# Mixture of experts on one core: leftover single tiles get units of their own at four fixed places

## The reference, cut to what matters

```
logits = flat @ gate_w.T                       # (4096, 8)
top_vals, top_idx = jax.lax.top_k(logits, 2)
top_w = jax.nn.softmax(top_vals, axis=-1)
for e in range(8):
    hdn = gelu(flat @ w1[e] + b1[e])           # 256 -> 1024
    out = out + combine[:, e:e+1] * (hdn @ w2[e] + b2[e])   # 1024 -> 256
```

## Time and profile before

| | us |
|---|---|
| median of 3 runs (lowest to highest) | 782.21 (781.34 to 785.01) |
| the profiled execution | 781.53 |
| its span, first to last instruction | 779.7 |
| stage A, about | 0 to 216 |
| stage B, about | 222 to 328.5 |
| stage C, about | 329.5 to 779.7 |
| PE busy over the span | 713.2 (91%) |

### The profile page before, as it was taken

How to read it: one execution, slowest core, us unless ns; L and a number is a source line. 1 busy time by engine, 2 the same in 40 slices (tenths; PEclk the granted TensorE clock), 3 DMA queues, 4 the chain that set the end, 5 groups by cost and what they waited for, 6 DMA issues and landing times.

```text
span 779.7 us, 18458 instructions
## 1 busy us (share of the span) xinstructions
PE 713.2 (91%) x5438; PEld 676.9 (87%) x5439; DVE 440.9 (57%) x1047; ACT 331.9 (43%) x640; POOL 407.9 (52%) x480
## 2 busy tenths in 40 slices
PE   5899999999948888489999999999999999999993
PEld 4899898998926666389999999999999999999993
DVE  3675756756636999735445455455454454454551
ACT  2673755747515677332323323323323223233230
POOL 1474565787662443273555546546555555555233
PEclk9999999999969999599999999999999999999997
DMA  7759568497460333224557536665576276273122
GB/s 243 247 174 398 208 264 359 163 333 252 171 271 28 111 110 109 84 75 120 170 156 229 178 55 206 186 176 148 155 246 166 41 237 175 48 229 77 19 29 30
DMA packets 45873, 130.14 MB, mean 167 GB/s; under 512 B 5185, under 2 KB 35521, under 8 KB 41217
## 3 DMA queue, kind: packets, MB, share of 16 engines
q1 hardware_dynamic: 30560, 104.86, 36.3%
q0 software_dynamic: 13904, 19.45, 14.6%
q10 hardware_dynamic: 1360, 5.24, 1.7%
HBM read 186.80 MB, written 47.59 MB: 301 GB/s over the span
## 4 chain that ended last, share of the span: by engine, by line
PE 55%; issue 1%; DMA 0%; POOL 0%; DVE 0%; ACT 0%; POOLq 0%; DVEq 0%
PE ps_h L73 9%; PE ps_h L74 9%; PE ps_h L75 9%; PE ps_y L73 8%; PE ps_y L75 8%; PE ps_y L74 8%; PE ps_x L1596 2%; PE ps_y L1589 1%; DMA out_tok<-y,to_row 0%; POOL out_tok L1471 0%; DVE xtl L1531 0%; DVE yb L1551 0%; DVE y L1558 0%; ACT xth L1496 0%; POOL to_row L1467 0%
## 5 line engine op out<-in xcount | busy, mean ns | idle before, releaser
L1505 ACT ACTIVATE g<-ps_h,bias 128x256 f32<-128x256 f32 x288 | 120.8, 471 | 277.7 <-PE ps_h L75 277.7
L1471 POOL DMA_INDIRECT out_tok<-y,to_row x72 | 126.9, 1763 | 137.7 <-DVE y L1558 117.2
L73 PE MATMUL ps_h<-xth,wbuf 128*128 128x256 f32 x576 | 163.2, 283 | 3.3 <-issue 1.8
L73 PE MATMUL ps_y<-wbuf,gl 128*128 x576 | 164.6, 286 | 0.0
L74 PE MATMUL ps_h<-xtl,wbuf 128*128 128x256 f32 x576 | 163.1, 283 | 0.0
L75 PE MATMUL ps_h<-xth,wbuf 128*128 128x256 f32 x576 | 161.8, 281 | 0.0
L75 PE MATMUL ps_y<-wbuf,gh 128*128 x576 | 161.7, 281 | 0.0
L74 PE MATMUL ps_y<-wbuf,gh 128*128 x576 | 161.7, 281 | 0.0
L73 PEld LDWEIGHTS ps_h<-xth,wbuf 128*128 128x128 f32 x576 | 108.0, 188 | 3.7 <-issue 2.1
L75 PEld LDWEIGHTS ps_h<-xth,wbuf 128*128 128x128 f32 x576 | 109.6, 190 | 0.0
L74 PEld LDWEIGHTS ps_y<-wbuf,gh 128*128 128x128 f32 x576 | 108.8, 189 | 0.0
(11 more groups left out here) (239 smaller groups left out, 1284.9 us busy)
## 6 DMA issues: line engine op xcount, KB each, us to landing
wbuf<-wsplit SPq DMA_DIRECT2D x71, 2048.0 KB, 8.1
wsplit<-wbuf SPq DMA_DIRECT2D x14, 2048.0 KB, 11.9
wraw<-in_w SPq DMA_DIRECT2D x16, 1024.0 KB, 7.9
raw<-in_x_ch ACTq DMA_DIRECT2D x5, 1024.0 KB, 8.8
normed<-x SPq DMA_DIRECT2D x8, 528.0 KB, 3.0
tok<-in_x_tok SPq DMA_DIRECT2D x1, 4096.0 KB, 16.7
out_tok<-tok SPq DMA_DIRECT2D x8, 512.0 KB, 3.7
x_rows<-normed,from_row POOLq DMA_INDIRECT x72, 3.4
```

The lines of the kernel that those rows point to most:

```text
L73: eng.matmul(out, ll, rh, start=first, stop=False)
L1471: pool.indirect_dma_start(out=out, out_offset=bass.IndirectOffsetOnAxis(ap=to_row[:, par, s:s + 1], axis=0), in_=y[:, par, s, :], in_offse ...
L1505: last = act.activation(g[:, f, :], ps_h[:, q, f % 2, :], ACT.Gelu_apprx_tanh, bias=bias1[:, bass.ds(e, 1), f:f + 1].rearrange("p a f -> p ...
```

## The change

Each expert's number of pairs becomes its count divided by 256 and rounded (count + 127, shifted by 8, at least 1), and where 1 to 128 tokens are left over, they are one **lone** tile. For the counts above: 3, 4, 4, 3, 4, 5, 5, 4 pairs = 32 and 1, 0, 1, 1, 0, 0, 0, 1 lone tiles = 4. The usual run still has 36 units, but every eighth (units 7, 15, 23 and 31) is a lone unit of one tile, whatever expert it belongs to, with both layers' weights in a buffer of its own, `lone_w` (128 x 8192 float32). It is filled in four transfers of a quarter during the first four units of each period of eight. What does not fit 32 pairs and 4 lone tiles runs in ten more units behind the branch. To make room, `x`, `g`, `y` and `yb` of stage C lie in the token buffer of the stages before. The loop body has eight units and runs three times.

```diff
+PERIOD = 8
+LONE = PERIOD - 1
+LONES = E // 2
+FULL = 2 * TOK // PAIR
+USUAL = FULL + LONES
...
 # stage B, SyncE: the second layers of experts 0 and 1 go to wsplit too
             sp.dma_start(bias1[:, :, :], b1_t).then_inc(biases_in, 16)
+            for e in range(2):
+                sp.dma_start(wsplit[e, :, W2AT:WROW], wbuf[:, e, W2AT:WROW].bitcast(F32)).then_inc(second_out, 16)
...
 # stage B, GpSimd: the pair number of each unit's place, three iotas for one
-                    (tile_id[:, :], [[1, PAIRS]], 0, 0),
+                    (by_period[:, :, 0:LONE], [[LONE, LONES], [1, LONE]], 0, 0),
+                    (by_period[:, :, LONE], [[LONE, LONES]], LONE - 1, 0),
+                    (tile_id[:, LONES * PERIOD:REST], [[1, REST - LONES * PERIOD]], LONES * LONE, 0),
...
 # stage C, SyncE
+            def lone_weights(u, at):
+                layer, n = at // 2, W2AT // 2
+                e = entry(sp, T_EXPERT, u + (LONE - at), E - 1)
+                cols = slice(at * n, (at + 1) * n)
+                sp.dma_start(lone_w[:, cols].bitcast(F32),
+                             wsplit[bass.ds(e, 1)].rearrange("a p w -> (a p) w")[:, cols]).then_inc(lone_in[layer], 16)
...
+                    if at < 4 and not (isinstance(u, int) and u + LONE - at >= USUAL):
+                        lone_weights(u, at)
...
+                    wait_apart(sp, lone_set, 1)
...
 # stage C, VectorE, ahead of the first x_low
+            def lone_table():
...
+                then(dve.tensor_scalar(lone_tiles_i[:, :], count_i[:, :], P.bit_length() - 1, None, ALU.arith_shift_right))
+                then(dve.tensor_copy(lone_tiles[:, :], lone_tiles_i[:, :]))
...
+                for i in range(1, PAIRS - USUAL + 1):
+                    then(dve.tensor_scalar(buffer_f[:, i:i + 1], buffer_f[:, i - 1:i], -1.0, 1.0, ALU.mult, ALU.add))
+                dve.tensor_copy(tabs[:, T_BUFFER, USUAL:PAIRS], buffer_f[:, 1:PAIRS - USUAL + 1]).then_inc(lone_set, 1)
...
+                if lo == 0:
+                    lone_table()
+                x_low(lo, lo % PERIOD)
...
 # stage C, TensorE
-                for s in range(2):
+                for s in range(rows_of(u, at) // P):
                     for k in range(KT):
                         last = pe.transpose(ps_x[:, k, s * P:(s + 1) * P], x[:, slot, s, k * P:(k + 1) * P], ident[:, :])
...
+                both = lone_w[:, 0:W2AT] if alone(u, at) else wbuf[:, par, 0:W2AT]
...
-                            last = mm3(pe, ps_h[:, q, f % 2, :], (wh[:, k, rows], wl[:, k, rows]),
-                                       (xth[:, par, k], xtl[:, par, k]), k == 0, k == KT - 1)
+                            last = mm3(pe, ps_h[:, q, f % 2, 0:n], (wh[:, k, rows], wl[:, k, rows]),
+                                       (xth[:, par, k, 0:n], xtl[:, par, k, 0:n]), k == 0, k == KT - 1)
...
-                for s in range(2):
+                for s in range(rows_of(u, at) // P):
                     rows = slice(s * P, (s + 1) * P)
```

More of the change, by code:

```diff
@@ L694, in _, with stage_b @@
             images(pe, image)
-def stage_b(nc, sem, tok, wbuf, wsplit, ident, fixed, xn, tabs, bias1, bias2, records, normed, b1_t, b2, out):
+def stage_b(nc, sem, tok, wbuf, wsplit, ident, fixed, xn, tabs, bias1, bias2, records, count_i, n_pairs, ends,
+            expert, expert_id, normed, b1_t, b2, out):
     with ExitStack() as ctx:
@@ L743, in stage_b @@
         empty = sb("empty", [P, CELLS])
[L745 to L749, removed]
+        pairs_i = sb("pairs_i", [P, E], I32)
+        past, picked = sb("past", [P, REST, E]), sb("picked", [P, REST, E])
+        passed, starts, first = sb("passed", [P, REST]), sb("starts", [P, REST]), sb("first", [P, REST])
+        expert_i = sb("expert_i", [P, REST], I32)
         ps_out = ps("ps_out", [P, B, HALF])
@@ L1190, in make_table @@
                 dve.memset(tabs[:, T_CHANGED, 0:1], 0)
                 dve.tensor_scalar(tabs[:, T_CHANGED, 1:2], expert[:, 1:2], 0.0, None, ALU.is_gt)
[L1192 to L1196, removed]
+                dve.tensor_tensor(tabs[:, T_CHANGED, 2:REST], expert[:, 2:REST], expert[:, 0:REST - 2], ALU.is_gt)
@@ L1198, in decode @@
+                then(dve.tensor_copy(expert_i[:, :], expert[:, 0:REST]))
+                dve.tensor_scalar(tabs[:, T_BUFFER, 0:REST], expert_i[:, :], 1, None, ALU.bitwise_and)
+                then(dve.scalar_tensor_tensor(out=tabs[:, T_FIRST, 1:REST], in0=expert[:, 1:REST], scalar=float(E - 1),
+                                              in1=first[:, 1:REST], op0=ALU.is_lt, op1=ALU.mult))
             def decode():
@@ L1322, with stage_c @@
 T_EXPERT, T_COLUMN, T_FIRST, T_NEXT, T_BUFFER, T_TOTAL, T_CHANGED = range(7)
-def stage_c(nc, sem, wbuf, ident, tabs, bias1, bias2, records, wsplit, normed, out):
+def stage_c(nc, sem, room, wbuf, ident, tabs, bias1, bias2, records, count_i, n_pairs, ends, pair_experts, expert_id,
+            wsplit, normed, out):
     with ExitStack() as ctx:
@@ L1351, in stage_c @@
         share_d = sem("c_share")
+        lone_w = sb("lone_w", [P, WROW], F32R)
+        lone_in = [sem(f"c_lone_w{i + 1}_in") for i in range(2)]
+        lone_set, lone_step = sem("c_lone_table"), sem("c_lone_steps")
+        lone_tiles_i, lone_tiles = sb("lone_tiles_i", [P, E], I32), sb("lone_tiles", [P, E])
+        lone_ends, lone_column = sb("lone_ends", [P, E]), sb("lone_column", [P, E])
+        lone_past, lone_hit = sb("lone_past", [P, E, E]), sb("lone_hit", [P, E, E])
+        lone_expert, lone_at = sb("lone_expert", [P, E]), sb("lone_at", [P, E])
+        lone_total, buffer_f = sb("lone_total", [P, 2]), sb("buffer_f", [P, PAIRS - USUAL + 1])
         xh_d, xl_d, g_d = sem("c_x_high"), sem("c_x_low"), sem("c_g")
@@ L1387, in all_pairs, with alone, rows_of, periods @@
                 run(USUAL, PAIRS)
+        def alone(u, at):
+            return at % PERIOD == LONE and not (isinstance(u, int) and u >= USUAL)
+        def rows_of(u, at):
+            return P if alone(u, at) else PAIR
+        def periods(u, at):
+            return u // PERIOD if isinstance(u, int) else (u - at % PERIOD) // PERIOD
         def later(u, step):
@@ L1394, in entry, with before, loads_of_first_layer @@
             return eng.value_load(tabs[0:1, row, bass.ds(u, 1)], min_val=0, max_val=top)
[L1396 to L1402, removed]
+        def before(u, at):
+            return u // SLOT if isinstance(u, int) else (u - at % SLOT) // SLOT
+        def loads_of_first_layer(u, at):
+            return before(u, at) * (SLOT // 2) + (at % SLOT + 1) // 2
         block = ctx.enter_context(nc.Block())
@@ L1447, in _, with gather @@
                 pool.sem_inc(s, CREDIT)
-            def gather(u, slot):
+            def gather(u, at):
+                slot = at % SLOT
+                if at == LONE and isinstance(u, int) and u == LONE:
+                    wait_apart(pool, lone_set, 1)
                 column = entry(pool, T_COLUMN, u, COLS - 2)
@@ L1556, in result @@
                 dve.wait_ge(share_d, done(u))
-                for s in range(2):
+                for s in range(m):
                     last = dve.tensor_scalar(y[:, par, s, :], yb[:, s, :], share[:, slot, s:s + 1], None, ALU.mult)
@@ L1597, in turn_x, with layer1 @@
                 last.then_inc(xt_mm, 1)
-            def layer1(u, slot):
-                par = slot % 2
-                wh, wl = [wbuf[:, par, i * W2AT // 2:(i + 1) * W2AT // 2].rearrange("p (k n) -> p k n", k=KT) for i in range(2)]
+            def layer1(u, at):
+                par, n = at % 2, rows_of(u, at)
+                both = lone_w[:, 0:W2AT] if alone(u, at) else wbuf[:, par, 0:W2AT]
+                wh, wl = [both[:, i * W2AT // 2:(i + 1) * W2AT // 2].rearrange("p (k n) -> p k n", k=KT) for i in range(2)]
                 if later(u, 1):
-                    pe.wait_ge(w1_in[par], loads_of_first_layer(u, slot) * 16)
+                    pe.wait_ge(w1_in[par], loads_of_first_layer(u, at) * 16)
+                if alone(u, at):
+                    pe.wait_ge(lone_in[0], periods(u, at) * 32 + 32)
                 pe.wait_ge(xl_d, done(u))
```

227 lines of the change are left out of this document (152 added, 75 removed).

## The result

The changed kernel takes 785.79 us in the median (784.25 to 787.46, 20 runs), the kernel before, in turn with it on the same chip, 783.15 us (780.52 to 785.2, 20 runs). The ratio is 1.0035, with a 95% interval of 1.0026 to 1.0043: slower by 2.6 us, where 768 us and a gain were forecast. The profiled execution of the changed kernel has a span of 783.5 us (before: 779.7).

A forecast was written before the change was run, and what follows sets the result against it. TensorE's queue was taken to bound stage C; 4 x (3.08 + 0.48) = 14.2 us saved, 0.3 + 0.2 + 0.1 = 0.6 added, turning 781.5 into 768 us, range 760 to 776.

The forecast's parts named there:

- the loop: Stage C's loop: eight units instead of four means fewer turns, TensorE has no idle time there, cost 0.
- its signs of being wrong: Narrow matmuls starting over 0.13 or under 0.09 us apart, or TensorE idling beside the lone units.
- Narrow matmuls: Layer 1 of a lone unit, 128 columns instead of 256: 0.109 us per matmul, 0.48 us saved per unit.
- columns count: Rival: lone-unit layer 1 time follows columns, 0.060 us per matmul, 758.5 us, half-way 763; chance 0.10.
- narrow is slow: Rival: lone-unit layer 1 matmuls take 0.215 us each, as two passes, ending at 788.2 us; chance 0.17.
- The transposes' pace: Unit 3's 128-column transposes, 0.109 us apart at full clock, taken as the pace of lone-unit layer 1 matmuls.
- The other row that was to carry this: L601's 24-column matmuls, 0.217 us apart, read as lower clock and halved to support a floor set by weights.
- A lone unit: TensorE in stage C: 3.08 us saved in layer 2 and transposes, plus 0.48 in layer 1, per unit.
- No wait beside the lone units: Stage C: GpSimd not late, 0.95 us to spare before unit 9, cost 0; rival of new waits 772 to 776, chance 0.07.
- Weights: Lone units' weight transfers, 4 MB per period: DMA share rises to about 0.7, nothing waits, cost 0.
- The table of lone tiles: 41 small VectorE instructions before the first x_low, 7.2 us mostly hidden: 0 to 0.5 us added, 0.3 taken.
- Stage B: Two more iotas and longer records 0.2 us, make_table's longer steps below 0.1 us; the two 2 MB stores 0.

The follow-up runs named there:

- the long loop alone: Kernel before, only its loop body changed to eight units run three times instead of four run seven times: 797.13 us, ratio 1.0176.
- its two runs with the hint: Changed kernel with TensorE told ahead that the loop's backward branch will be taken, measured twice: 771.78 us (0.9864) and 771.24 us (0.9857).
- With the two missed terms out of the way: Changed kernel with TensorE told ahead of the loop's backward branch, and without the ten spare units and their branch: 768.72 us, ratio 0.9830.

## Why the prediction was wrong

**The step that failed** is the loop: it "has fewer turns; in the stretch of seven turns PE has no idle time, so 0". The rows were read rightly, but they belong to a body of four units. That a body twice as long goes back as cheaply was taken over from them without a bound. It costs 13.7 us by medians in the long loop alone, and about 14 as the difference between the changed kernel and its two runs with the hint. No rival named it, and the range had no room for it. Nor did any of its signs of being wrong come up: they watched the lone units' matmuls and waits, and not the loop. The short taken branch (0.25 us at most) shows what a branch costs when the code is at hand, and nothing of the case when it isn't. But a branch of microseconds stood in the trace before all the same, on the engine that sets the time: TensorE's own jump over the three spare units, at the end of its program, where nothing waits for it.

```profile
L1386 PEldq COMPARE_BRANCH  x1: 4076/4076/4076, 765.0 to 765.0; - x1
```

It took 4.1 us (after, over ten units, 4.2), where the same engine's taken branches in the loop of four took at most 0.25. No run here takes this jump apart, but as a bound for two ways back it gives an estimate of up to 8 us, before any loss by the clock, and not 0.

**A term was left out**: the jump over ten spare units instead of three at the end of GpSimd's program, 2.3 us in the trace. Taking all spare units out gives 2.5 back by medians and 2.9 in the trace, of which 0.6 is in the kernel before as well (7.7 against 7.1 us from the last scatter to the end).

**The rest of the sum held.** Saved between units 3 and 35, once the way back is hinted: 379.62 - 365.39 = 14.23 us, against 14.2 forecast. Its parts:
- Narrow matmuls: 0.111 us against 0.109, with nothing of "columns count" or "narrow is slow" in them, and 0.44 us saved per lone unit against 0.48. The transposes' pace was the right row to take. The other row that was to carry this does not: L601 was read as running at the lower clock, and half its 0.217 us was taken. But the trace before has the granted clock at 1.00 there (start and end of the stretch, then as in the rows above):

```profile
7.50:9.10 1.60, 1.55 (x8) 1.55 (x8) 0.45 (x3) 1.50 (x2) 0.00 (x0) 1.00 0.86 249
```

So this row doesn't support the halving, nor the agreement of L601's pace with 107 ns. The weight loads do (0.33 us here against 0.19 in stage C); which of the two is right stays open, and the forecast stands on the transposes alone.
- A lone unit: 3 x 11.863 - 32.14 = 3.45 us less than a full one, against 3.56. The missing 0.4 us over four are made good by full units that take 11.83 instead of 11.863. No run here shows the reason, so that the whole comes out at 14.23 is partly luck.
- No wait beside the lone units: with the halved layer 2 of unit 7 it is 445.36 - 436.35 = 9.01 us from unit 9's transposes to unit 10's (forecast 9.0), and from 445 to 746 us PE's idle time is in the two holes alone. The view of PE's waits, after (waited for: us in total, times, longest):

```profile
PE ps_h L79 <- issue: 8.7, 2, 4.4
```

- Weights: the DMA share is 0.67 to 0.71 up to 590 us, as forecast, and 0.53 behind it (0.51 to 0.57 before), a quarter of `lone_w` lands in 6.4 us, a `wbuf` load in 9.0 instead of 8.1, and nothing waits for either. DMA issues after (KB each, median us to landing):

```profile
wbuf<-wsplit SPq DMA_DIRECT2D x71, 2048.0 KB, 9.0
...
lone_w<-wsplit SPq DMA_DIRECT2D x16, 1024.0 KB, 6.4
```

- The table of lone tiles: 0 instead of 0.3 us. DVE's timeline after, the table's first and last instruction and the `xtl` behind them:

```profile
331.92 0.17 DVE L1614 TENSOR_TENSOR tabs<-pair_experts 128x3 int32<-128x3 f32 x1 [1.10 <-PEq L717]
...
338.07 0.17 DVE L1654 CAST tabs<-buffer_f 128x10 int32<-128x10 f32 x1
339.08 0.69 DVE L1659 TENSOR_TENSOR xtl<-ps_x,xth 128x512 fp32r<-128x512 f32 x1 [0.84 <-ACT xth L1560]
```

It takes 6.3 us instead of the 7.2 forecast (331.92 to 338.07 + 0.17), and is done 0.84 us early. From `records` to this `xtl` it is 330.40 to 339.08, 8.68 us, and 8.76 before.
- Stage B: from the last attention matmul of stage A to `records` 112.3 to 113.7 us in the seven traces that have the change, 112.4 to 112.5 in the three that don't: -0.1 to 1.3 us, where 0.3 was forecast. These runs don't settle it closer.

With the two missed terms out of the way, the change measures 768.72 - 782.45 = -13.7 us, and the sum was -13.6. Less the 0.6 us that the three spare units cost only the kernel before, it is about -13.1; an agreement closer than that would be luck, since stage B alone is open by more than a microsecond. So the direction hung on one step costed at nothing. What stays open: the changed kernel without spare units is about 5 us faster than with them, by medians from two sessions. The profiled executions differ by 4.5 us, of which 2.9 lie at the end and 1.5 before unit 3, where traces of one kernel vary by as much (the two with the hint by 2.3).

## What to carry to other kernels

A longer loop body can bring a cost that the shorter one doesn't have: a row of a short loop without idle time bounds nothing for a longer one. So give the way back a bound from both sides, look for a branch of microseconds anywhere on the engine that sets the time, and hint the branch or write that engine's units out. The same goes for code that is only jumped over, where the engine that ends last does the jump. Where a change brings a different control flow along, try the control flow alone first: here it was an edit of four lines, and it had 13.7 us of the error in it, which was 16.2 (2.6 measured, -13.6 forecast).

## What was not expected of the hardware

- In three traces, one way back to the start of a loop of eight units cost 4.1 to 5.1 us of idle TensorE, and with the lower clock after it 5.9 to 7.1; the same loop with the hint, or a loop of four units without it, none, at branches of 0.26 us or less. VectorE, ScalarE, GpSimd and SyncE, with far fewer instructions in the same loop, had branches under 0.08 us.
- A jump over code cost GpSimd 2.5 us where ten units were skipped (2.6 and 2.8 with the hint) and 0.1 where three were (0.5 in the long loop alone), outside the branch's own 0.05. On TensorE the jump's own row is long in both: 4.2 and 4.1 us.
- From `xtl` of unit 0 to `xtl` of unit 2 the ten traces take 16.4 to 16.5, 17.9 to 18.0 or 19.4 to 19.5 us, whichever the kernel. The granted clock from 348 to 352 us is 1.00 in the three traces of the first group and 0.57 to 0.84 in the others; what decides it no run here shows. The comparisons of traces above therefore start at unit 3.
